# Attention A: a tile's position rows written in two halves of 64 rows, without their unread columns, with operand loads between the two writes

## What is computed

```python
content_score = jnp.einsum('bhsp,bhtp->bhst', q + u, k)
pos_score = jnp.einsum('bhsp,htp->bhst', q + v, pos)
pos_score = _relative_shift(pos_score)
score = (content_score + pos_score) / jnp.sqrt(jnp.float32(P))
weights = jax.nn.softmax(score, axis=-1)
out = jnp.einsum('bhst,bhtp->bhsp', weights, val)
```

```python
def _relative_shift(x):
    b, h, s, _ = x.shape
    x = jnp.pad(x, ((0, 0), (0, 0), (0, 0), (1, 0)))
    x = x.reshape(b, h, s + 1, s)
    return x[:, :, 1:, :].reshape(b, h, s, s)
```

## Time and profile before

| | us |
|---|---|
| median of three runs | 9972.04 |
| the profiled execution | 9952.2 |
| its span, first to last instruction | 9950.4 |
| TensorE busy | 8953.0 (90%) |
| VectorE busy | 6015.3 (60%) |
| ScalarE busy | 5584.0 (56%) |
| GpSimd busy | 2779.5 (28%) |

### The profile page before, as it was taken

How to read it: one execution, slowest core, us unless ns; L and a number is a source line. 1 busy time by engine, 2 the same in 40 slices (tenths; PEclk the granted TensorE clock), 3 DMA queues, 4 the chain that set the end, 5 groups by cost and what they waited for, 6 DMA issues and landing times. The chain is left out here.

```text
span 9950.4 us, 256407 instructions
## 1 busy us (share of the span) xinstructions
PE 8953.0 (90%) x91488; PEld 5835.1 (59%) x91488; DVE 6015.3 (60%) x12530; ACT 5584.0 (56%) x10811; POOL 2779.5 (28%) x2894
## 2 busy tenths in 40 slices
PE   6988999899899899989989989998998999999899
PEld 4666666445566666644556666664555666666445
DVE  4666664664466666467456666646745666663673
ACT  4666664454466666445446666634545666663454
POOL 3333332100333333210033333321003333332101
PEclk8999999899899999989989999998998999999899
DMA  8999994110799999321079999922108999992110
GB/s 311 406 389 394 402 405 163 68 35 24 283 406 397 394 403 398 146 72 33 24 305 404 395 391 406 401 120 73 32 24 329 404 400 394 405 400 97 67 36 24
DMA packets 440127, 2552.03 MB, mean 256 GB/s; under 512 B 60017, under 2 KB 90225, under 8 KB 176369
## 3 DMA queue, kind: packets, MB, share of 16 engines
q1 hardware_dynamic: 438768, 2534.40, 64.6%
HBM read 1284.53 MB, written 1248.85 MB: 255 GB/s over the span
## 5 line engine op out<-in xcount | busy, mean ns | idle before, releaser
L830 POOL TENSOR_SCALAR z<-z,nmax 128x1024 f32<-128x1024 f32 x2048 | 2270.3, 1120 | 3648.5 <-DVE nmax L779 3648.5
L769 DVE CUSTOM_DVE_ANT_0 z<-sc,z 128x1024 f32<-128x1024 f32 x2048 | 2496.2, 1219 | 1182.8 <-DMA z<-rel_rows 1172.3
L726 ACT ACTIVATE rel<-rg 128x512 f32<-128x512 f32 x3072 | 1722.0, 596 | 1590.6 <-PE rg L603 879.8
L731 ACT ACTIVATE pT<-rg 128x512 f32<-128x512 f32 x4096 | 2226.1, 595 | 517.4 <-PE rg L636 516.8
L636 PE MATMUL rg<-ident,z 128*128 128x128 f32 x16384 | 2182.6, 277 | 3.7 <-ACT pT L731 3.2
L636 PEld LDWEIGHTS rg<-ident,z 128*128 128x128 f32 x16384 | 1781.4, 142 | 503.1 <-issue 360.4
L1080 ACT ACTIVATE pT<-rg 128x512 f32<-128x512 f32 (+3 forms) x2560 | 1226.0, 531 | 827.0 <-PE rg L1012 498.0
L1096 DVE TENSOR_REDUCE mx_b<-sc 128x1 f32<-128x1024 f32 (+7 forms) x1024 | 1004.0, 991 | 466.6 <-PE sc L994 231.2
L657 PE MATMUL op<-pT,xnT 128*32 128x128 f32 x32768 | 1121.7, 278 | 4.0 <-DVE rel L808 3.2
L802 DVE COPY rel<-rg 128x512 f32<-128x512 f32 x1024 | 708.4, 692 | 457.0 <-PE rg L607 424.9
L989 PE MATMUL sc<-z 96*128 96x512 bf16 (+3 forms) x2560 | 764.9, 370 | 145.4 <-DMA z<-k_parts 70.0
(11 more groups left out here) (115 smaller groups left out, 8867.1 us busy)
## 6 DMA issues: line engine op xcount, KB each, us to landing
rel_rows<-rel SPq DMA_DIRECT2D x1024, 1088.0 KB, 9.1
z<-rel_rows SPq DMA_DIRECT2D x1024, 1024.0 KB, 9.6
v_heads<-rel SPq DMA_DIRECT2D x8, 4096.0 KB, 12.7
xnT<-v_heads SPq DMA_DIRECT2D x128, 256.0 KB, 4.3
qu_parts<-z SPq DMA_DIRECT2D x36, 512.0 KB, 4.4
pos_s<-pos_parts SPq DMA_DIRECT2D x64, 192.0 KB, 9.4
qv_parts<-z SPq DMA_DIRECT2D x24, 512.0 KB, 7.6
k_parts<-z SPq DMA_DIRECT2D x24, 512.0 KB, 5.2
```

The lines of the kernel that those rows point to most:

```text
L726: e.activation(rel[:, r % RING, c * CH:(c + 1) * CH], rg[:, R_BANK[c], :], ACT.Copy).then_inc(r_copied[c], 1)
L731: e.activation(pT[:, t % 2, q * CH:(q + 1) * CH], rg[:, T_BANK[q], :], ACT.Exp, scale=SCALE).then_inc(p_ready[q], 1)
L769: e.tensor_tensor_reduce(out=zs, in0=scf[:, 2 * half * CH:2 * (half + 1) * CH], in1=zs, scale=1.0, scalar=-3.0e38, op0=ALU.add, op1=ALU.ma ...
L830: e.tensor_scalar(zs, zs, 1.0, nmax[:, n % 2:n % 2 + 1], ALU.mult, ALU.add).then_inc(AA[done], 1)
```

## The change

The one write of a tile becomes two, of 64 rows (`SH`) each. Half 0 (rows 0 to 63) writes columns 64 to 2175, half 1 (rows 64 to 127) columns 0 to 2111: 2112 columns or 8448 B a row instead of 8704 B, 528 KB a half. The columns left out are read by no row of that half. The waits for the copies stay ahead of half 0 (`rows_ready`). The step's operand loads, with their own waits, are issued after half 0, and half 1 after them. A tile's writes now add 32 to `rel_out`, so those who wait for it count by `written`; `moved` stays for the reads.

```diff
+SH = P // 2
...
+        def written(base, n):
+
+            return base.writes + 16 * (P // SH) * (n // RING + 1)
...
-                        e.wait_ge(rel_out[r % RING], moved(base, r - RING))
+                        e.wait_ge(rel_out[r % RING], written(base, r - RING))
...
-            def write_rows(base, n):
-
-                k, hd, i0 = n % RING, n // NT % NB, n % NT * P
+            def rows_ready(base, n):
+
                 for c in (R_DVE, R_ACT[-1]):
                     e.wait_ge(r_copied[c], e.snap(base.tiles + (n + 1)))
                     settle(e)
                 e.wait_ge(tail_copied, e.snap(base.tiles + (n + 1)))
                 settle(e)
-                there = bass.AP(tensor=rel_d.tensor, offset=hd * FLAT + i0 * W, ap=[[W, P], [1, W]])
-                e.dma_start(there, rel[:, k, :]).then_inc(rel_out[k], 16)
+
+            def write_rows(n, g):
+
+                k, hd, i0 = n % RING, n // NT % NB, n % NT * P + g * SH
+                c0 = P - SH - g * SH
+                there = bass.AP(tensor=rel_d.tensor, offset=hd * FLAT + i0 * W + c0, ap=[[W, SH], [1, S + SH]])
+                e.dma_start(there, rel[g * SH:(g + 1) * SH, k, c0:c0 + S + SH]).then_inc(rel_out[k], 16)
...
                 if here(r):
-                    write_rows(base, r)
+                    rows_ready(base, r)
+                    write_rows(r, 0)
                 if s >= 0:
                     next_heads(p, base, s, final)
                 else:
                     second_head(s)
+                if here(r):
+                    write_rows(r, 1)
```

More of the change, by code:

```diff
@@ L92 @@
 ROWS = dict(bv=0, bo=1, Bbv=2, Bbo=3, b2=4)
-Counts = namedtuple("Counts", "tiles fours moves pairs values")
+Counts = namedtuple("Counts", "tiles fours moves pairs values writes")
 Marks = namedtuple("Marks", "heads blocks pieces groups pairs values rows steps")
@@ L572, in counts @@
                 return Counts(*(e.snap(b * (nh // HB * per) + p * per)
-                                for per in (G, G // OB, 16 * G // RING, HB // NB * QK_INC, HB // NB * 16)))
+                                for per in (G, G // OB, 16 * G // RING, HB // NB * QK_INC, HB // NB * 16, 16 * (P // SH) * G // RING)))
             with e.Fori(0, 1) as p:
@@ L877, in read_ready @@
                     settle(e)
-                e.wait_ge(rel_out[k], e.snap(moved(base, n)))
+                e.wait_ge(rel_out[k], e.snap(written(base, n)))
                 settle(e)
```

## The result

The changed kernel took 10574.61 us (median), the kernel before 9970.53 us beside it: a ratio of 1.0602, 95% interval [1.059, 1.0615], or 604 us slower. The profiled execution has a span of 10572.4 us.

What follows compares the result with a forecast made beforehand. DMA engines were taken to bound attention A, TensorE just behind. 9952 us plus 1946 for half the partitions (shorter rows counted) plus 25 for the second DMA made 11,923, stated as 11,900 us; range 9,870 to 12,500.

Steps and rivals of the forecast that it cites:

- The bound: In attention A the DMA engines bind, 5.24 us a tile at 413 GB/s, with TensorE 2% behind at 5.13 us.
- Bytes removed: Attention A's writes: 32 KB less a tile saves 0.079 us, 81 us over 1024 tiles, or zero if TensorE keeps all.
- One more DMA: A second write DMA a tile: SyncE's 335 us of issues covered by waits; 25 us on the DMA engines, between 0 and 51.
- What is moved: Operand loads between the halves delay half 1 and the next read; cost nothing while the queue holds work.
- Half of the partitions: Half writes in attention A run at about half rate, 222 GB/s: 1.9 us more a tile, between zero and 2.20.
- The dips of the earlier trace: Rate dips to 381 GB/s beside operand-load pairs, read as the pair taking 1.18 us instead of 0.63, half the rate.
- The sum by that page: At the page's limit of 218 GB/s a tile's write would take 4.96 us, 2.29 us more than now.
- The second: Rival: half writes cover one another in part, +0.57 us a tile, 583 us, 10,535 us in all; chance 0.20.
- The first: Rival: stores out of 64 partitions run like those out of 128, only bytes count, 9871 to 9922 us; chance 0.19.
- the third rival: Half a tile's partitions cost nothing, but TensorE at 98% takes the whole 81 us gain, 9940 to 9960 us; chance 0.03.
- The profile that I had named: Attention A at 290 to 310 GB/s instead of 400; VectorE's wait for rows read back from 1172 to about 3000 us.
- The clock: TensorE's clock may fall as it waits; at 0.8 a tile needs 6.4 us; left at nothing, 250 us for the upper end.

Runs made afterwards that it cites:

- the two kernels with halves: Changed kernel (10574.61 us) and the same with all 2176 columns in each 64-row half write, 32 KB a tile more: 10613.24 us, ratio 1.0648.
- short rows: Kernel before, its one 128-row write cut to 2112 columns, in rows of 2112 for write and read: 9908.2 us, ratio 0.9944.
- odd and even rows: Changed kernel with each of the two writes taking every second row, all 2176 columns, spanning all partitions: 10128.88 us, ratio 1.0153 to the kernel before.
- the series: Kernel before, with stores and loads of tiles in several forms timed behind its end: 16 stores whole 42.6 us, in halves of 64 partitions 53.4 us.
- column halves together: Against the kernel before, two writes of all 128 rows, half the columns each, issued back to back ahead of the operand loads: 10058.45 us, ratio 1.0085.
- one write: Kernel before with its whole 128-row write issued behind the operand loads in steps that have them: 9984.36 us, ratio 1.0013.
- half 0 alone: Transfers using only partitions 0 to 63, timed behind the end of the kernel before: stores 204 GB/s, loads 202 GB/s.
- half 0 twice: Changed kernel with both half writes out of partitions 0 to 63: 10858.61 us, ratio 1.0912; as 16 tiles stored behind the kernel before: 88.0 us.

## Why the prediction was right or wrong

- **The bound** was read rightly: the loss lies in attention A and in the DMAs, 574 of 622 us between its first and last reads. The sign followed from it, against a change that moves fewer bytes.
- **Bytes removed**: 81 us forecast, 60 measured, 39 between the two kernels with halves. That TensorE, at 98%, kept the rest is not shown: the DMA share from 300 to 1450 us is 1.00 with short rows as before.
- **One more DMA**: I took 25 us between 0 and 51; it is 88 with rows in two packets, and 161 with its place for odd and even rows, whose rows stay whole. The bound came from a DMA share of 1.01. But the share also reads 1.0 at 202 GB/s, so it cannot show that nothing is lost. That DMAs do not each cost this much on the DMA engines is seen in the series, where odd and even rows store at 418 against 421 GB/s. SyncE, which I had covered with its waits, is held longer at each issue. In column halves together that did not starve the DMA engines, whose share from 300 to 1450 us stayed at 1.00; the time there is in packets, the 66 us above and reads of 348 instead of 340 ns a row. Why the reads are slower beside two writes stays open.
- **What is moved**: nothing forecast, 14 us for one write, 40 to 55 us for two. Why two writes pay more was not tested.
- **Half of the partitions** is the step that failed, and the term is mis-sized by a factor of three to four: 1.9 us a tile forecast, 0.47 to 0.59 measured. The rate of 222 GB/s was right, for stores too: alone, 204. Wrong was to let it stand for every byte of the write. I had named what speaks for less, that engines which are through with half 0 work beside those that are not, and set it aside since the operand loads were hardly covered. The series shows what that cover is worth: stores in halves cost 0.68 us a tile alone and 0.52 us with a load behind each, not 2.2.
- **The dips of the earlier trace rows** were also misread. They were real, but the time was not lost in the operand loads. In 3540 to 3546 us the packets of the pair (4096 B) took 180 ns on average against a median of 159 from 300 to 1450 us; the reads' rows took 382 ns instead of 309. Over all 16 engines that is 0.07 us lost in the loads and 0.59 us in the reads. So the pair did not run at half its rate, as the term assumed; it slowed the reads beside it, and no row showed that this grows with the bytes of a write. Why a pair of loads costs the reads as much as that for its few bytes, and half writes so much less, is open.
- **The Trainium skill.** The page "SBUF — State Buffer", section "Door 1: The DMA port swizzle", gives 218 GB/s for 64 partitions; the stores and the loads of half 0 alone, 204 and 202 GB/s, come within 8% of it. That two DMAs on the two halves gain only 6%, in its section "Can I just issue two DMAs to hit both halves?", agrees with the loads here (223 against 202, 10%) and not with the stores (358 against 204, 75%). The sum by that page would have missed as mine did.
- **The rivals.** The second was right in sign and size: 583 us forecast, 604 measured. The agreement is partly luck, since its 0.65 us for the partitions and nothing for the rest stand against 0.5 us and 128 us. Its picture, engines that slow each other only while they are at the same half, is borne out by half 0 twice, which is slower, and by the series: stores in halves alone take 53.4 us instead of 42.6, the quarter more that it forecast. It had no slower reads, which are the larger part in the kernel. That the engines drift apart, and by how much, was not seen; no view here tells one DMA engine from another. The first and the third rival fell: stores out of partitions 0 to 63 run at half the rate, and the time moved by 604 us.
- **The profile that I had named**: GB/s fell to 345 to 367, not 300, and VectorE's wait rose to 1478 us, not 3000. The rate said "second rival" at once; the wait rose by 306 us, about half of what a third of my figure would be.
- **The clock** was left at nothing, and that is not shown. The granted clock over a run fell from 0.961 to 0.934, and TensorE, with the same instructions, was busy 216 us longer. From 300 to 1450 us it was busy 5.4 of 6.28 us a tile, so it did not bind on average. But the DMA engines were without a packet for 0.11 us a tile, and whether a slower TensorE has a part in that was not tested.

## What to carry to other kernels

A transfer out of or into partitions 0 to 63 alone runs at half the rate here, whichever way it goes, while 64 rows spread over all partitions run at the full one. What it costs in a stream depends on what is beside it, and the neighbours pay too: here the whole reads lost more than the half writes. So price it in a stream with the same neighbours, not from a burst, and when the rate dips, look whose packets got longer before you say whose price it is. Splitting a transfer costs by itself, here 88 to 161 us for 1024 more DMAs, depending on how it is split and what stands between, although the DMA share read 1.0 and SyncE had waits to spare; that is more than the 3% of a write's bytes that the split saved. If a write has to be split in two, a split by columns or by odd and even rows keeps all partitions in each and is 480 to 500 us better here than a split into halves with the same bytes.

## What was not expected of the hardware

The DMA share does not fall when packets take longer: 1.00 at 202 GB/s and 1.00 at 425. Only the GB/s beside it tells, or the duration of the packets, 334 ns a stored row with whole stores and 674 ns with half 0 twice. Stores in alternating halves reached 358 GB/s and loads in alternating halves 223, though half 0 alone is at half the rate both ways; why stores part and loads do not is open.
